# Mamba scan: two of sixteen products with C moved from VectorE to GpSimd, with three product buffers and a ring of four states

## The reference, cut to what matters

```
dA = exp(dt_t[..., None] * A)
h = dA * h + (dt_t * u_t)[..., None] * B_t[:, None, :]
y = einsum('bcn,bn->bc', h, C_t)        # per step
y = (ys + u * Dp) * silu(z); out = y @ wo.T
```

## Time and profile before

| | |
|---|---|
| median of 3 runs | 2419.44 us (2419.38 to 2421.32) |
| profiled execution, its time | 2414.19 us |
| its span, first to last instruction | 2412.4 us |
| DVE busy | 1678.4 us, 70% |
| PE busy | 1885.5 us, 78% |
| ACT busy | 1199.8 us, 50% |
| POOL busy | 1059.7 us, 44% |

### The profile page before, as it was taken

The page is one execution under the profiler, slowest core; times in us unless marked ns, Lnnn a source line. Parts: engine busy times, 40 slices in busy tenths (PEclk is TensorE's granted clock), DMA queues, the critical chain, the costliest instruction groups (busy, mean ns, idle before and its releaser), DMA issues. The chain is left out here.

```text
span 2412.4 us, 50985 instructions
## 1 busy us (share of the span) xinstructions
PE 1885.5 (78%) x19950; PEld 1386.9 (57%) x19950; DVE 1678.4 (70%) x2554; ACT 1199.8 (50%) x2657; POOL 1059.7 (44%) x811
## 2 busy tenths in 40 slices
PE   4788888988888764667728788577667499999997
PEld 2344444444433323445528777456656499999997
DVE  1599999999999964457484442335534588888886
ACT  2767776777676542023415444232525155555554
POOL 0377777776777740610007777000620033333332
PEclk8898999999999995567769999687878699999998
DMA  2444444444445411500128887102710521122000
GB/s 71 124 129 131 132 146 129 130 133 125 126 133 146 128 47 39 102 17 1 33 74 245 257 257 218 47 0 90 240 46 13 168 58 58 58 58 58 4 4 21
DMA packets 121948, 241.07 MB, mean 100 GB/s; under 512 B 16428, under 2 KB 72054, under 8 KB 121182
## 3 DMA queue, kind: packets, MB, share of 16 engines
q1 hardware_dynamic: 107261, 212.37, 29.2%
q0 software_dynamic: 9408, 18.93, 3.7%
q10 hardware_dynamic: 5040, 6.52, 0.8%
HBM read 222.46 MB, written 15.30 MB: 99 GB/s over the span
## 5 line engine op out<-in xcount | busy, mean ns | idle before, releaser
L874 POOL TENSOR_TENSOR dBu<-du,Bs 128x858 f32<-128x858 f32 (+1 forms) x240 | 588.3, 2453 | 228.5 <-DVE hst L798 101.1
L395 PE MATMUL py<-hst,ident 128*128 128x429 f32 (+1 forms) x960 | 418.9, 568 | 93.5 <-DVE hst L808 93.0
L798 DVE TENSOR_TENSOR_SCAN hst<-dA,dBu 128x858 f32<-128x858 f32 (+1 forms) x240 | 457.9, 1908 | 22.6 <-ACT dA L690 21.7
L1866 POOL DMA_INDIRECT xi<-token_rows,take x152 | 148.2, 975 | 544.7 <-POOLq L90 499.3
L690 ACT ACTIVATE dA<-dt,negA 128x416 f32<-128x416 f32 (+1 forms) x480 | 269.6, 596 | 182.6 <-DVE hst L798 181.5
L395 PEld LDWEIGHTS py<-hst,ident 128*128 128x128 f32 x960 | 185.7, 205 | 293.2 <-DVE hst L808 165.0
L2397 POOL TENSOR_TENSOR hm<-h,mw 128x264 f32<-128x264 f32 x128 | 107.2, 838 | 452.0 <-DVE h L2378 452.0
L808 DVE TENSOR_TENSOR hst<-hst,Cs 128x858 f32<-128x858 f32 (+1 forms) x240 | 246.7, 1028 | 0.0
L2337 ACT ACTIVATE z<-pg,scale 128x136 f32<-128x136 f32 (+2 forms) x512 | 207.4, 488 | 45.4 <-PE pg L2304 43.6
L2304 PE MATMUL pg<-xm,wi 128*128 128x68 f16 x6144 | 216.6, 195 | 1.9 <-issue 1.9
L2304 PE MATMUL pg<-hs,wh 128*128 128x68 f16 x6144 | 215.3, 195 | 1.8 <-issue 1.8
(11 more groups left out here) (400 smaller groups left out, 3204.1 us busy)
## 6 DMA issues: line engine op xcount, KB each, us to landing
wb<-sf_w SPq DMA_DIRECT2D x96, 514.0 KB, 4.9
Bs<-bc_rows SPq DMA_DIRECT2D x96, 429.0 KB, 4.7
Cs<-bc_rows SPq DMA_DIRECT2D x96, 429.0 KB, 3.5
mw<-route_weights SPq DMA_DIRECT2D x8, 2112.0 KB, 15.8
wb<-gf_w SPq DMA_DIRECT2D x24, 514.0 KB, 4.9
Bs<-bc_rows SPq DMA_DIRECT2D x24, 396.0 KB, 5.1
Cs<-bc_rows SPq DMA_DIRECT2D x24, 396.0 KB, 4.3
mb<-route_masks SPq DMA_DIRECT2D x8, 1088.0 KB, 6.9
```

The costliest lines, as they stand in the source:

```text
L395: return nc.tensor.matmul(out, weight, moving, **kw)
L798: v.tensor_tensor_scan(hst[:, g % HR, 0:2 * n], dA[:, g % 2, 0:2 * n], dBu[:, g % 2, 0:2 * n], 0.0, ALU.mult, ALU.add).then_inc(h_ready, 1)
L874: g_.tensor_tensor(dBu[:, g % 2, 0:2 * n].rearrange("p (a n) -> p a n", a=2), du[:, j % 2, :, 0:n], Bs[:, q % NBS, k % BG, 0:n].unsqueeze( ...
L1866: pool.indirect_dma_start(xi[:, j % UN, :], None, xs, bass.IndirectOffsetOnAxis(ap=take[:, j:j + 1], axis=0)).then_inc(taken[j % UN][0], 16)
```

## The change

Three edits. The product with C of states 4 and 12 of each item moves from DVE to POOL, in place, issued by POOL before its product with B three states later (`weigh(g - 3)`), with a semaphore of its own (`weighed_pool`) that PE and SP wait for. `dBu` gets three buffers, and POOL's product with B waits for scan g-3 instead of scan g-2. The ring of states `hst` has four places instead of five, so scan g waits for PE's addition of state g-4.

```diff
-HR = 5
+HR = 4
+DB = 3
+POOL_STATES = (4, 12)
+
+def weighed_by(g):
+
+    p = sum(k in POOL_STATES for k in range(g % DST + 1)) + g // DST * len(POOL_STATES)
+    return g + 1 - p, p
...
-        dBu = sb("dBu", [128, 2, 2 * SCW])
+        dBu = sb("dBu", [128, DB, 2 * SCW])
...
                     if q >= NBS:
-                        sp.wait_ge(weighed, BG * (q - NBS + 1))
+                        sp.wait_ge(weighed, weighed_by(BG * (q - NBS + 1) - 1)[0])
+                        if weighed_by(BG * (q - NBS + 1) - 1)[1] > 0:
+                            sp.wait_ge(weighed_pool, weighed_by(BG * (q - NBS + 1) - 1)[1])
...
-                pe.wait_ge(weighed, g + 1)
+                if k in POOL_STATES:
+                    pe.wait_ge(weighed_pool, weighed_by(g)[1])
+                else:
+                    pe.wait_ge(weighed, weighed_by(g)[0])
...
-                v.tensor_tensor_scan(hst[:, g % HR, 0:2 * n], dA[:, g % 2, 0:2 * n], dBu[:, g % 2, 0:2 * n], 0.0, ALU.mult,
+                v.tensor_tensor_scan(hst[:, g % HR, 0:2 * n], dA[:, g % 2, 0:2 * n], dBu[:, g % DB, 0:2 * n], 0.0, ALU.mult,
...
-                if g >= 1:
+                if g >= 1 and (g - 1) % DST not in POOL_STATES:
                     weigh(g - 1)
...
+            def weigh(g):
+                j, k = g // DST, g % DST
+                l, at, n = item(j)
+                q = g // BG
+                pool.wait_ge(c_loaded[q % NBS], 16 * (q // NBS + 1))
+                pool.wait_ge(h_ready, g + 1)
+                h = hst[:, g % HR, 0:2 * n].rearrange("p (a n) -> p a n", a=2)
+                g_.tensor_tensor(h, h, Cs[:, q % NBS, k % BG, 0:n].unsqueeze(1).broadcast_to([128, 2, n]),
+                                 ALU.mult).then_inc(weighed_pool, 1)
...
+                if (k - 3) % DST in POOL_STATES and g >= 3:
+                    weigh(g - 3)
                 if g % BG == 0:
                     pool.wait_ge(b_loaded[q % NBS], 16 * (q // NBS + 1))
-                if g >= 2:
-                    pool.wait_ge(h_ready, g - 1)
-                g_.tensor_tensor(dBu[:, g % 2, 0:2 * n].rearrange("p (a n) -> p a n", a=2), du[:, j % 2, :, 0:n],
+                if g >= DB:
+                    pool.wait_ge(h_ready, g - DB + 1)
+                g_.tensor_tensor(dBu[:, g % DB, 0:2 * n].rearrange("p (a n) -> p a n", a=2), du[:, j % 2, :, 0:n],
```

More of the change, by code:

```diff
@@ L327, in mamba_lstm @@
             stage(nc, "d_ready e_abs d_read e_ready ser_ready ln_ready marked ser_done patched dt_done du_done"))
-        (dA_zeroed, dBu_ready, dA_ready, h_ready, weighed, y_added, y_gated) = ctx.enter_context(
-            stage(nc, "dA_zeroed dBu_ready dA_ready h_ready weighed y_added y_gated"))
+        (dA_zeroed, dBu_ready, dA_ready, h_ready, weighed, weighed_pool, y_added, y_gated) = ctx.enter_context(
+            stage(nc, "dA_zeroed dBu_ready dA_ready h_ready weighed weighed_pool y_added y_gated"))
         (wop_ready, wop_kept, cent_ready, cent_kept, sq_ready, var_ready, var_kept, var_logged, rstd_ready, m_scaled, m_done) = ctx.enter_context(
```

## The result

The changed kernel takes 2441.61 us (median of 4 runs, 2436.42 to 2447.11); before it is 2420.38 us (4 runs beside them, 2419.38 to 2425.01). The ratio is 1.0091, 95% interval 1.0076 to 1.0105: slower by 18 to 25 us. The forecast was 2441 us.

What follows compares the result with a forecast made beforehand. DVE, busy 768 of 785 us in the scan stage, was taken as the bound, with POOL excluding its two-SBUF-input products. Collisions less gains gave +22.3 us: 2414.2 becomes 2436.5, plus 5.2 for the median, about 2441; range 2407 to 2457.

Steps and rivals of the forecast that it cites:

- No wait for POOL to remove, and the third buffer costs: Scans never wait for POOL; POOL ahead after k = 10 delays product 9: +0.8 us per LSTM item, +1.5 otherwise.
- Product 12 on POOL: Behind k = 12, DVE's product 13 loses 1.6 us against 0.94 gained: +0.65 an item, -0.94 in the last.
- Product 4 hides behind ACT: Product 5 loses 1.07 us against 0.94 gained, both hidden in the wait before scan 8: -0.2 per LSTM item.
- ACT's waits absorb part: DVE's existing waits for ACT take up losses: 0.32 us at scan 12 in LSTM items; 0.44 idle at scan 8.
- The ring costs nothing: Scan g waits for PE's addition of state g-4, with 0.7 us to spare at the tightest; 0 charged.
- The sum: LSTM items +13.8 us and the others +8.5, together +22.3 us on the profiled execution.
- Rival 1: POOL's products do not hold DVE off, so the moves pay: -19 us, 2400 us; chance 0.13.
- Rival 2: Only wide collisions are lost; margins of 0.1 to 0.2 us go DVE's way: -5.7 us, 2414; chance 0.17.
- Rival 3: More losses than walked, at product 8, the ring and `dBu`: +10 to +18 us on top, 2451 to 2459; chance 0.16.

Runs made afterwards that it cites:

- buf3: Kernel before with three product buffers and a ring of four, no product moved: 2436.98 us against 2423.06, ratio 1.0053.
- buf3_gate: As buf3, but POOL's product with B waits for scan g-2 again: 2421.70 us against 2422.62 before, ratio 0.9998.
- ring4: Kernel before with only the ring cut from five places to four: 2423.40 us against 2423.06, ratio 1.0005.
- move12: As ring4, with two product buffers and only product 12 moved to POOL: 2429.96 us against 2419.64 before, ratio 1.0046.
- move4: As ring4, with two product buffers and only product 4 moved to POOL: 2420.75 us against 2419.64 before, ratio 1.0008.
- fill_b: The change, with POOL writing a constant into `dBu` in place of the product with B: 2399.43 us against 2419.64 before, ratio 0.9915.

## Why the prediction was right, point by point

- *No wait for POOL to remove, and the third buffer costs.* Right, shown by buf3 and buf3_gate. At k = 9 the forecast loss was 1.12 us in an item with an LSTM cell; measured in item 5: 1.99 - 1.03 = 0.96. From the length of product 9 in all items the mean is 1.09, and 1.6 in the four others (1.63 forecast). The third buffer was put at 15 us; 13 measured against before, 10.5 by the stage against ring4.
- *Product 12 on POOL.* About the right sum by another way. The walk had POOL 0.15 us ahead at k = 13. With three buffers DVE is ahead by 0.02 to 0.04 us there in every item but the last, where nothing behind k = 12 is lengthened, as forecast. The term that was sized wrong is POOL's product with C: it ends 1.88 us behind DVE's product (408.38 to 410.26 in item 5) and not 1.71, so POOL comes to k = 13 later by 0.16 us, and the lead of 0.15 is gone. The collision comes one or two states later. The text gave that case but let the series run on to the gating at k = 1 and a loss of 0.3 us; it ends in a collision of 1.48 us on average, in all 14 items (1.6 forecast for k = 13). That the loss came out nearly the same is luck. With two buffers (move12) POOL is ahead by 0.02 to 0.13 us at k = 13, in every item, the last included.
- *Product 4 hides behind ACT.* The time is right: move4 is level with before. The place is not. The forecast had gain and loss disappear in the wait before scan 8; move4's scans wait 3.7 us less than ring4's, and it is the LSTM instruction at k = 5 that waits 6.6 us more for ACT. The chain of ACT that scan 8 waits for was also read from scan 5 on, and it starts at scan 2. Product 5 takes 0.9 us more in the LSTM items (1.07 forecast), from 0.2 to 1.4. In the four others the collision came in two items only, at product 6, where the forecast had four.
- *ACT's waits absorb part.* The terms of the forecast give them 8.8 us: 4.1 at scan 12, 4.7 at scan 8. The scans' waits became 5.9 us shorter, and the wait of the LSTM instruction at k = 5 became 2.1 us longer.
- *The ring costs nothing.* Right within the interval of ring4, -2 to +5 us.
- *The sum.* The products are longer by 267.8 - 210 x 1.028 = 51.9 us, and 30 starts of 0.94 give back 28.2. The waits of the scans for ACT and PE give back 6.4, and that of the LSTM instruction costs 2.1. That leaves 19.4, against +17.3 of the stage; 2 us are not placed. The forecast was +22.3, all of it in the stage, with collisions of 59.4 us in place of 51.9. The largest part of that is product 4 (18.2 forecast, 13.0 measured: two collisions fewer, the others smaller), then product 12 (22.4 and 20.9) and the third buffer (18.8 and 18.5). Against it stands that ACT's waits absorbed less.
- *The closeness of 2441.* It is luck in part. The stage grew by 17.3 us, 5 less than forecast; the rest of the program was 4.9 us longer in the profiled execution, which the forecast did not foresee and which the change does not touch. The mechanism of the collisions was right; the wait that hides product 4 and the way of product 12 were not.
- *Rival 1* said what would be left without the collisions: 2400 us; fill_b took them away and measured 2399.4. It also took away the few that the kernel before has (3.7 us), and its scans wait 26.9 us for ACT against 21.7 before, so the agreement is no proof of each term. *Rival 2* had close margins go DVE's way. At k = 13 they did, but the loss behind that was 1.5 us and not 0.3. *Rival 3*'s collisions in every other item at product 8 came once, not in seven items, and only in buf3.

## What to carry to other kernels

Before work is moved from VectorE to GpSimd, count the time in which either engine reads two SBUF tensors, for both engines together: here the product with C and the product with B take 1.03 + 1.71 us of a period of 2.80, so a move makes it longer (1.03 becomes 1.7 to 2.0) and there is no room. This is an estimate from the lengths; move12 bears it out, one product moved and nothing else changed from ring4. Look for the place where VectorE works from PSUM or on small tiles, and put the moved work there: one product at k = 1 gained 10 us of the stage, one at k = 12 lost 9 (move12 against ring4). A buffer count can be what keeps two engines in step; a deeper queue on an engine that nobody waits for lets it arrive first.

## What the runs showed of the hardware

- Who is first holds the other off, down to small margins: POOL at 410.50 against DVE at 410.52 made a 1.03 us product take 2.74 us; DVE at 411.99 against POOL at 412.02 kept its 1.02 us. Within 0.03 us the recorded starts do not tell who wins. In the changed kernel's first item POOL is recorded 0.02 us ahead of DVE's product 8 (at 125.60), and that product still takes 1.03 us.
- The Trainium skill ("SBUF — State Buffer", § Who interferes with whom) has it that the order of issue decides who blocks; the traces agree but for margins of under 0.03 us, and put the release 0.10 to 0.12 us ahead of the recorded end of POOL's instruction in all 306 cases.
- A product on DVE that waits shows the wait as its own length, in `busy`, with 0.0 us of idle before it: no view of waits names it. The mean length of a group against that in another kernel is where it is seen.
- A DVE product with one input in PSUM, begun under a running product of POOL, kept its 1.03 to 1.05 us in all 132 cases.
- The in-place product with C takes 2.00 us on POOL when nothing is beside it for states 4 and 12, 1.84 to 1.86 for state 1 and 1.69 to 2.01 for state 0 (858 elements). Why it differs by place was not looked into.
- POOL's memset of 858 elements takes 0.81 us, beside a product of DVE too.
